# Full-array turns set between the tile pairs of two gathers, with 7, 6 and 3 pairs per gather in place of 6, 5 and 5

## The reference, cut to what matters

```python
x = x + L0(gn(x))     # Fourier modes along rows and columns, plus a 1x1 mix of the channels
x = x + L1(gn(x))     # deformable 3x3 convolution

# L1, per image: om = conv3x3(x, w_om) + b_om gives 27 values for each pixel
off, mask = om[:, :18], sigmoid(om[:, 18:])        # 9 taps: dy, dx and a mask
vals = bilinear_sample(x, ys + dy, xs + dx) * mask # 9 samples of each channel at each pixel
out  = einsum('bckhw,ock->bohw', vals, weight) + bias
```

## Time and profile before

| | us |
|---|---|
| median of 3 runs | 1885.19 (1885.1 to 1886.07) |
| the profiled execution | 1881.98 |
| its span, first to last instruction | 1880.0 |
| PE busy | 1710.9 |
| DVE busy | 1397.7 |
| ACT busy | 1119.3 |
| GpSimd busy | 890.8 |

### The profile page before, as it was taken

The page is one execution under the profiler, slowest core; times in us unless marked ns, Lnnn a source line. Parts: engine busy times, 40 slices in busy tenths (PEclk is TensorE's granted clock), DMA queues, the critical chain, the costliest instruction groups (busy, mean ns, idle before and its releaser), DMA issues.

```text
span 1880.0 us, 160529 instructions
## 1 busy us (share of the span) xinstructions
PE 1710.9 (91%) x71037; PEld 1328.0 (71%) x71037; DVE 1397.7 (74%) x2196; ACT 1119.3 (60%) x1858; POOL 890.8 (47%) x1153
## 2 busy tenths in 40 slices
PE   8475507899999999999999999999999999999986
PEld 3241105688888888888888888888888888888874
DVE  8959914577777777777777777777777777777773
ACT  0001344577777777777777777776666767667662
POOL 1000004455555555555555555555555555555550
PEclk9779957999999999999999999999999999999997
DMA  9014753233333333333333333333333333333320
GB/s 374 20 59 167 297 222 91 72 93 93 93 93 93 93 92 93 92 93 92 93 93 97 93 90 88 92 91 91 91 91 93 92 93 93 93 93 93 93 77 13
DMA packets 161676, 195.94 MB, mean 104 GB/s; under 512 B 20288, under 2 KB 136672, under 8 KB 157536
## 3 DMA queue, kind: packets, MB, share of 16 engines
q1 hardware_dynamic: 161632, 195.34, 35.0%
HBM read 143.05 MB, written 52.22 MB: 104 GB/s over the span
## 4 chain that ended last, share of the span: by engine, by line
PE 84%; DVE 6%; issue 5%; DVEq 2%; DMA 2%; ACT 1%; SPq 0%; ACTq 0%
PE pE L989 18%; PE pVV L1069 16%; PE pE L1010 13%; PE pM L1035 10%; PE pVV L1010 8%; PE pR L1023 7%; PE pVV L1023 7%; PE pM L1045 4%; DVE big L722 3%; DMA xh_scratch<-win 1%; DVEq L722 1%; DVE stats L657 1%; PE pVV L941 1%; DVE sums L655 1%; ACT win L557 1%
## 5 line engine op out<-in xcount | busy, mean ns | idle before, releaser
L495 POOL COPY big<-win 128x480 f32<-128x480 f32 x520 | 289.6, 586 | 641.0 <-PE pVV L1023 457.8
L483 POOL TENSOR_TENSOR prod<-big 128x600 f32<-128x600 f32 (+1 forms) x489 | 498.6, 1041 | 29.6 <-POOL big L516 29.5
L749 DVE COPY big<-pE 128x768 f32<-128x768 f32 x390 | 372.9, 956 | 104.0 <-PE pE L989 91.0
L586 ACT ACTIVATE big<-pE 128x768 f32<-128x768 f32 x390 | 334.4, 858 | 177.1 <-PE pE L989 177.1
L755 DVE STREAM_TRANSPOSE big<-prod 128x768 f32<-128x768 f32 x390 | 377.4, 968 | 3.6 <-POOL prod L483 3.6
L989 PE MATMUL pE<-big,sel_s 32*64 32x192 f32 x12480 | 356.2, 336 | 6.2 <-DVE big L749 4.9
L1069 PE MATMUL pVV<-big,wc 64*32 64x128 f32 x18720 | 294.3, 272 | 3.8 <-issue 2.8
L989 PEld LDWEIGHTS pE<-big,sel_s 32*64 32x64 f32 x12480 | 219.1, 132 | 108.3 <-issue 56.6
L1069 PEld LDWEIGHTS pVV<-big,wc 64*32 64x32 f32 x18720 | 262.2, 106 | 45.9 <-issue 45.9
L1010 PE MATMUL pE<-big 60*32 60x72 f32 x20800 | 254.8, 231 | 15.4 <-issue 15.4
L1010 PEld LDWEIGHTS pE<-big 60*32 60x32 f32 x20800 | 234.0, 105 | 22.1 <-issue 16.9
(11 more groups left out here) (81 smaller groups left out, 1731.4 us busy)
## 6 DMA issues: line engine op xcount, KB each, us to landing
big<-xh_scratch SPq DMA_DIRECT2D x390, 136.0 KB
win<-xh_scratch SPq DMA_DIRECT2D x130, 408.0 KB, 3.7
xh_scratch<-win SPq DMA_DIRECT2D x32, 544.0 KB, 2.7
big<-in_x SPq DMA_DIRECT2D x16, 1024.0 KB, 15.6
x_scratch<-big SPq DMA_DIRECT2D x16, 1024.0 KB, 3.9
x1r<-x_scratch SPq DMA_DIRECT2D x256, 64.0 KB, 3.0
out<-outs SPq DMA_DIRECT2D x256, 64.0 KB, 2.1
xh_scratch<-zero SPq DMA_DIRECT2D x4, 204.0 KB, 2.7
```

What stands on the lines that cost most here:

```text
L483: made = nc.gpsimd.tensor_tensor(prod[:, kx, at:at + m, 0:SQ].rearrange("p m (a b) -> p m a b", a=NSH), hy.to_broadcast(shape), hx.to_broa ...
L495: last = nc.gpsimd.tensor_copy(strips[:, half * HTP:(half + 1) * HTP, h, 0:REG].rearrange("p t (r x) -> p t r x", r=WIN_R), tiles_of(q, h, ...
L586: nc.scalar.activation(*expanded(kx, 0), ACT.Copy).then_inc(e_read, 1)
L749: nc.vector.tensor_copy(*expanded(kx, 1)).then_inc(e_read, 1)
```

## The change

Three things change. The 16 tile pairs are split 7, 6 and 3 over the gathers. On PE, `gather` gets a hook `between`, called after each tile pair but the last of its gather: in the first gather it puts the second and third offset turn after the third and fifth pair, in the second gather the four transposes of `turn_rows(N + 1, 0)` after the first four pairs. Only the first offset turn stays ahead of the gathers, and `turn_rows(N + 1, 0)` no longer stands behind them. On ACT the copy of that turn moves from behind the three `samples` to between the first and the second.

```diff
-VGROUPS = [(0, 6), (6, 11), (11, 16)]
+VGROUPS = [(0, 7), (7, 13), (13, 16)]
@@ ScalarE, step
                 if on[0]:
-                    for gi in range(NG):
-                        samples(N, gi)
+                    samples(N, 0)
                 if on[1]:
                     turned(N + 1, 0)
+                if on[0]:
+                    samples(N, 1)
+                    samples(N, 2)
+                if on[1]:
                     turned(N + 1, 1)
@@ TensorE, gather
-            def gather(n, gi):
+            def gather(n, gi, between=None):
...
+                    if between and t < t1 - 1:
+                        between(t - t0)
                 last.then_inc(v_done, 1)
...
+            def turn_first(n):
+
+                def one(t):
+                    if t == 0:
+                        wait_rows(n, 0)
+                    if t < TPC:
+                        turn_tile(0, t)
+                return one
...
-            def turn_offsets(n):
-
-                pe.wait_ge(om_act, n + 1)
+            def turn_offsets(f):
...
-                for i, m0, m1 in FILLS:
-                    last = mm(o[:, :, m0:m1], om_s[:, i * W:(i + 1) * W], place_of[:, :, m0:m1],
-                              start=True, stop=True)
-                last.then_inc(omT_done, 1)
+                i, m0, m1 = FILLS[f]
+                last = mm(o[:, :, m0:m1], om_s[:, i * W:(i + 1) * W], place_of[:, :, m0:m1],
+                          start=True, stop=True)
+                if f == len(FILLS) - 1:
+                    last.then_inc(omT_done, 1)
+
+            def turn_last(t):
+
+                if t in (2, 4):
+                    turn_offsets(t // 2)
@@ TensorE, step
                 if on[3]:
-                    turn_offsets(N + 3)
+                    pe.wait_ge(om_act, N + 4)
+                    pe.nop(nofuse=True)
+                    turn_offsets(0)
+                    if not on[0]:
+                        turn_offsets(1)
+                        turn_offsets(2)
                 if on[0]:
-                    for gi in range(NG):
-                        gather(N, gi)
+                    gather(N, 0, turn_last if on[3] else None)
+                    gather(N, 1, turn_first(N + 1) if on[1] else None)
+                    gather(N, 2)
                 if on[1]:
-                    turn_rows(N + 1, 0)
+                    if not on[0]:
+                        turn_rows(N + 1, 0)
                     turn_rows(N + 1, 1)
```

More of the change, by code:

```diff
@@ L1011, in gather, with wait_rows @@
                                   A[part, b * NTP + t, :], start=True, stop=True)
+                    if between and t < t1 - 1:
+                        between(t - t0)
                 last.then_inc(v_done, 1)
             def turn_rows(n, k):
+                wait_rows(n, k)
+                turn_tiles(k)
+            def turn_first(n):
[5 more added lines that the diff above has]
+                return one
+            def wait_rows(n, k):
                 wait(pe, xt_done, n * TCH + k - k % 2)
@@ L1021, in turn_rows, with turn_tiles, turn_tile @@
                     wait(pe, conv_read, n)
+            def turn_tiles(k):
                 for u in range(TPC):
[L1023 to L1026, removed]
+                    turn_tile(k, u)
+            def turn_tile(k, u):
+                last = nc.tensor.transpose(pT[k][:, u * P:(u + 1) * P],
+                                           strips[:, k * TPC + u, :, :].rearrange("p h x -> p (h x)"),
+                                           ident[:, :])
+                if u == TPC - 1:
+                    last.then_inc(t_done, 1)
             def offsets(n):
```

## The result

The change made the kernel slower: 2128.3 us median (2126.98 to 2129.3) against 1885.14, a ratio of 1.1289 with a 95% interval of 1.1273 to 1.1306. The prediction was 2141 us with a range of 2076 to 2205. The profiled span is 2126.4 us, 246.4 more than before.

The account below looks back on a forecast made before the run. PE was taken as the bound, draining at each change of weight form. Terms 1.28 + 1.10 - 0.36 - 0.035 + 0.01 gave +2.00 us a step, +256 us in all, so 2141 us, range 2076 to 2205.

Parts of the forecast that it names:

- four transposes, from gather matmul to gather matmul: Second gather: each transpose put between tile pairs takes 0.44 us from gather matmul to gather matmul, where 0.01 is normal.
- two offset turns, the same way: First gather: each inserted offset turn, two records, takes 0.56 us, 0.55 over normal spacing; +1.10 us a step for two.
- behind the gathers, with the spread's wait: After the last gather: four transposes fewer in a row save 0.44 us; the spread's wait adds 0.01.
- The price of a border: TensorE drains at each change of weight form, 12 more a step; next load 0.07 us before record end, matmul 0.03 later.
- The pile of issued instructions: Gathers: tile pairs after a pause take 0.13 us, not 0.18; 12 of 16 instead of 4, -0.36 us a step.
- The 0.38 us of the offset turns ahead of the gather: Ahead of the first gather: the 0.38 us freed becomes PE idle time behind ACT's copy into pVV; counted as nothing.
- The convolution's wait: Spread to convolution: with ACT's first copy moved earlier, the wait ends ahead of the drain, -0.035 us a step.
- the spread's: Next step's first spread waits for the last gather to be emptied: +0.01 us a step, bounds 0 and +0.15.
- The count of steps: Whole kernel: 127 steps pay all of +2.00 us, two more the transposes alone at +1 each, together +256 us.
- A: Borders between forms: the semaphore wait drains, not the form; about -0.05 us a step, 1879 us; chance 0.08.
- B: Inserted turns: gather to transpose drains, the way back doesn't; 1.0 us a step left, 2012 us; chance 0.05.
- C: Gather's stretch: the clock falls to 0.50 for a quarter of each step, 2450 us; chance 0.03.

Follow-up runs that it names:

- e1: The changed kernel with its three offset turns in a row ahead of the first gather again, only the four transposes inside the second gather: 2015.29 us, ratio 1.0694.
- e2: The changed kernel with the next step's transposes behind the gathers again, only two offset turns inside the first gather: 1988.9 us, ratio 1.055.
- e5: As e1, but each transpose made by four matmuls of the gather's own form, turning half the channels' partitions (not the reference): 1904.91 us, ratio 1.0111.
- e4: As e1, but all four transposes in one block after the second gather's first pair: 1920.25 us, ratio 1.0189.
- e6: The kernel before with 36 columns in each gather matmul in place of 72 (does not compute the reference): 1855.87 us, ratio 0.9845.

## Why the prediction was right

The mechanism held at each of the places named, and the sum was off by 13 of 243 us. Term by term, for one step, from the table and the record starts behind it:

| term | predicted | measured |
|---|---|---|
| four transposes, from gather matmul to gather matmul | 4 x 0.44 = 1.76 | 4 x 0.411 = 1.64 |
| two offset turns, the same way | 2 x 0.56 = 1.12 | 2 x 0.510 = 1.02 |
| the 16 tile pairs themselves | -0.36, -0.06 for normal spacings counted above | 2.56 for 2.80: -0.24 |
| behind the gathers, with the spread's wait | -0.44 + 0.01 | 0.790 - 1.176 = -0.39 |
| from the spread to the gather | -0.035 | 7.772 - 7.823 = -0.05 |
| sum | +2.00 | +1.98 |

(The tile pairs' 2.56 is 2.104 + 3.120 less the insertions, their 2.80 is 1.088 + 1.712.)

- *The price of a border* was read right, and a little too high. I had put the matmul 0.03 us behind its load, as at 1008.73 behind 1008.70 in the earlier trace rows; but that is how it stands where the load had waited. Behind a drain alone it starts within 0.003 (1010.95 and 1010.95 above). Six times 0.03 is the 0.22 less in the first two rows, with an offset turn's second spacing of 0.15 for 0.17.
- *The pile of issued instructions* gave back 0.18 and not 0.36 (0.24 and 0.42 with the 0.06 of normal spacings). The count was right: by the medians 12 of the 16 pairs take 0.11 to 0.15 us. But right behind a used-up pile the issue is slower than its mean of 0.18 a pair: the four others take 0.21 to 0.26. The last five pairs, 80 records that start from 1012.58 to 1013.44 (1.08 - 0.22), show it: they take 0.86, and three at 0.13 to 0.15 leave 0.44 for two. I had taken the mean for all. This error and the one before nearly cancel, so that the sum came out at 1.98 for 2.00 is in part luck.
- *The 0.38 us of the offset turns ahead of the gather* gave nothing, as said: ACT's copy ended the wait, and PE was idle for 0.35 us in its place. In the text on what would show it I had also written that PE stays busy throughout; that did not fit with this step, and the window says 389.88 of 400 us, which is 29 steps with 0.35 idle.
- *The convolution's wait* went (0.901 to 0.840), and *the spread's* came: 0.05 us more than the drain alone, where I said 0.01. It is DVE's copy (L747) that ends it, as the sum assumed.
- *The count of steps.* The profiled spans differ by 246.4 us, where the forecast had 256. The fourth step's first spread starts at 353.1 us before and at 352.4 after: the first three steps, in which PE has pauses of up to 2.9 us, paid nothing in place of 6. From there 124 steps add 244.7 us, 1.97 each, and the last two, which have the transposes alone, with the end of the kernel 2.4. The rest of the miss is that the profiled execution before lay 3.2 us under its median and the one after did not.

The rivals: A (it is the wait that drains, and not the form) is ruled out by the borders with no wait behind them that drain in full, 0.07 us from load to end of record, and by what e1 and e2 cost. e5 doesn't speak against a drain by waits as such: there a wait with a nop inside an unchanged form stopped PE too. B (half a drain) is ruled out by 1011.49, the load behind a transpose, 0.07 before its end. C (the clock) is ruled out by the granted clock of 1.00. That full-array weights have to wait for any matmul under way, whatever its form, is ruled out by the earlier trace rows: from turn to turn they load 0.28 before the end of the run.

Of the rule of the Trainium skill (TensorEngine Tiling (Array Packing), Key Properties) that a change of the tiling mode drains the engine, e1 and e4 are a direct measurement here: 0.15 us for each change between 64-row by 32-column and full-array weights, 0.13 with the faster pairs behind it taken off. The rule that weight loads are pulled ahead (TensorE: Matmul & The Clock Gate, Part 2, Step-by-step) shows here within a form, with loads 0.14 and 0.28 us before the end of the run in the earlier trace rows; across a change of form no load came more than 0.073 before it in any step from 600 to 1750 us of the nine kernels.

## What to carry to other kernels

Count the changes of form of the weights on TensorE's list as a cost of its own: here 0.15 us each (0.13 net), more than a whole 128x128 transpose (0.109). Keep matmuls of one form together, and look for the price in the distance from the end of a run to the next weight load (here 0.07 us or less: drained; 0.09, in e6, to 0.28: not), since the busy share stays at 90% and hides it. A distance clearly under 0.07, as in e5, says that something beside the form holds the load back. Before work is moved ahead of or behind a wait, ask what that wait is for: the 0.38 us of offset turns taken off the list ahead of the first gather went whole into the wait for ACT's copy.

## What the runs showed of the hardware that was not expected

- The gather has two paces: 8 ns a record while instructions are piled up from a pause (some 32 records with their loads), then 11 ns on the mean, and 14 to 17 directly behind the pile. Half the columns took some 16% off the first pace and 7% off the second (e6).
- The price of a change of form did not depend on how long the run on either side is: one transpose alone takes 0.411 us from gather matmul to gather matmul, four in a block 0.739, which less three spacings of 0.109 is 0.412. The load stands 0.07 us before the end of the record in both.
- A wait with a nop between matmuls of one form emptied PE as a change of form does (e5): 0.237 us from matmul to matmul, where the other three turns of the step start 0.01 to 0.03 us behind a gather matmul.
